# Two bias rows written into PSUM by ScalarE, and a reordered last stage, in a two-layer graph network kernel

## What is computed

```
xn = layernorm(x)
support = ((xn @ U) * s) @ Vt                                # rank 64
g  = relu(segment_sum(support[col] * val, row) + bias)       # L1_gnn_bias
q  = softmax over each head; k = softmax over the nodes
m  = (q @ (k^T v per head)) @ w_proj + b_proj                # L1_mix_b_proj
x  = x + g + m
ll, lh, hl, hh = haar(layernorm(x))
h  = gelu(interpolate(ll) @ fc1^T + fc1_b)
x  = x + inverse_haar(h @ fc2^T + fc2_b, lh, hl, hh)
```

## Time and profile before

| | |
|---|---|
| median of 3 runs | 594.62 us |
| the profiled execution | 594.25 us |
| its span, first to last instruction | 592.5 us |
| PE / DVE / ACT / POOL busy in it | 550.9 / 474.2 / 326.2 / 289.6 us |
| granted PE clock | full speed throughout (1.0) |

### The profile page before, as it was taken

The page is one execution under the profiler, slowest core; times in us unless marked ns, Lnnn a source line. Parts: engine busy times, 40 slices in busy tenths (PEclk is TensorE's granted clock), DMA queues, the critical chain, the costliest instruction groups (busy, mean ns, idle before and its releaser), DMA issues.

```text
span 592.5 us, 8690 instructions
## 1 busy us (share of the span) xinstructions
PE 550.9 (93%) x2921; PEld 443.8 (75%) x2921; DVE 474.2 (80%) x1037; ACT 326.2 (55%) x614; POOL 289.6 (49%) x321
## 2 busy tenths in 40 slices
PE   2988989998999999999999998999998999999997
PEld 1776877775877777888887665878876788778787
DVE  7689989888999778757898878768767786677996
ACT  7767868767764672122214765556436786423242
POOL 3747677676778705635661694000503565021553
PEclk9999999999999999999999999999999999999999
DMA  9400000000002020102204001000002000020004
GB/s 319 154 2 1 1 1 2 1 1 2 0 2 72 2 71 18 37 19 82 38 14 139 15 9 63 0 1 1 1 2 88 1 0 2 2 90 1 1 0 175
DMA packets 15046, 21.12 MB, mean 36 GB/s; under 512 B 3260, under 2 KB 6000, under 8 KB 15002
## 3 DMA queue, kind: packets, MB, share of 16 engines
q1 hardware_dynamic: 13674, 17.94, 9.6%
q10 hardware_dynamic: 1328, 2.62, 1.2%
HBM read 18.00 MB, written 2.56 MB: 35 GB/s over the span
## 4 chain that ended last, share of the span: by engine, by line
PE 58%; DVE 20%; issue 8%; POOL 6%; ACT 4%; DMA 3%; DVEq 1%; ACTq 0%; SPq 0%; POOLq 0%
PE p L2197 10%; PE pQ L2317 4%; PE p L2032 4%; PE p L2317 4%; DVE onehot L1374 3%; POOL qx L1183 2%; PE pH L2209 2%; PE pQ L2048 2%; DVE p L1472 2%; PE p L2282 2%; PE pQ L2515 2%; PE pH L2515 2%; PE pQ L2209 2%; PE pH L2048 2%; POOL xT L1171 2%
## 5 line engine op out<-in xcount | busy, mean ns | idle before, releaser
L999 POOL TENSOR_TENSOR Loh<-onehot,whl 128x512 fp32r<-128x512 f32 x85 | 89.4, 1052 | 47.6 <-DVE onehot L1374 47.6
L1374 DVE TENSOR_SCALAR onehot<-iota_src,srclo 128x128 fp32r<-128x128 f32 x170 | 74.7, 479 | 0.7 <-DVE flagint L1386 0.7
L2032 PEld LDWEIGHTS p<-Roh,Loh 128*128 128x128 f32 x340 | 47.6, 190 | 31.6 <-issue 27.7
L2197 PE MATMUL p<-G,ATs 128*128 128x512 f32 x300 | 70.5, 391 | 0.0
L2197 PEld LDWEIGHTS p<-G,ATs 128*128 128x128 f32 x300 | 55.9, 188 | 11.6 <-issue 0.2
L2032 PE MATMUL p<-Roh,Loh 128*128 128x200 f32 x340 | 53.2, 279 | 11.7 <-POOL Loh L999 4.9
L566 ACT ACTIVATE away<-iota_key,key 128x200 f32<-128x200 f32 x85 | 38.7, 456 | 24.2 <-PE p L2032 24.2
L2048 PE MATMUL pQ<-wsl,xT 128*128 128x512 f32 x168 | 47.5, 412 | 2.4 <-DVE xT L1288 2.4
L2048 PE MATMUL pH<-wsl,xT 128*128 128x512 f32 x168 | 45.4, 398 | 0.0
L568 ACT ACTIVATE Roh<-away,onesf 128x200 fp32r<-128x200 f32 x85 | 39.3, 463 | 2.8
L1405 DVE TENSOR_TENSOR AT<-AT,p 128x200 f32 x85 | 30.0, 353 | 13.2 <-PE p L2032 8.4
(11 more groups left out here) (650 smaller groups left out, 1440.7 us busy)
## 6 DMA issues: line engine op xcount, KB each, us to landing
xb<-in_x SPq DMA_DIRECT2D x9, 256.0 KB, 2.6
out<-nodes SPq DMA_DIRECT2D x9, 256.0 KB
wraw<-in_L_mix_w_qkv ACTq DMA_DIRECT2D x2, 1024.0 KB, 7.7
raw<-in_L_mix_w_qkv SPq DMA_DIRECT2D x2, 1024.0 KB, 5.2
nodes<-in_x SPq DMA_DIRECT2D x1, 1024.0 KB, 8.9
wraw<-in_L_mix_w_qkv SPq DMA_DIRECT2D x1, 1024.0 KB, 11.3
wraw<-in_L_gnn_W SPq DMA_DIRECT2D x1, 1024.0 KB, 13.5
raw<-in_L_mix_w_out SPq DMA_DIRECT2D x1, 1024.0 KB, 5.2
```

The costliest lines, as they stand in the source:

```text
L999: pool.tensor_tensor(Loh[:, g % SLOTS], o, w, ALU.mult).then_inc(S["oh_pool"], 1)
L1374: ins = v.tensor_scalar(onehot_[:, g % SLOTS, c, :], iota_src[:], srclo[:, 2 * g + c:2 * g + c + 1], None, ALU.is_equal)
L2032: ins = pe.matmul(pW[g % 2][:, 0:T * WIN], Loh[:, g % SLOTS, c, part, :], Roh[:, g % RSLOTS, c, :], start=(c + part == 0), stop=(c + part ...
L2197: ins = pe.matmul(pG[u][:, :], ATs[:, u, x, s_, :], G[:, y, s_, :], start=(s_ + n == 0), stop=(s_ == T - 1 and n == 2))
```

## The change

It does seven things, all in the second layer.

1. `b2` becomes a plain float32 tile with both bias rows on all 128 partitions, by two broadcast transfers of 256 KB in place of two of 4 KB. DVE's three preparing instructions and a POOL memset go.
2. The 4 bias matmuls behind `kT . Wp` and the 10 in `support` go. ACT copies a bias row into the PSUM bank (`support_bias`, `mix_bias`, 128x512, 10 of each), and the products accumulate on it (`start=False`). PE waits for these copies (`pg_ok`, `pm_ok`).
3. On ACT the copies of tile t+2 stand right behind `r2_hi(t + 2)`, and wait for `x3_ok` of tile t.
4. `gelu` of groups 1 and 2 writes back into its PSUM bank, and its doubling reads from there.
5. `doubled(0)` on ACT moves behind `sums_hi(1)`; `gelu_lo(0)` moves from DVE (before `sums_lo(1)`) to POOL, between pair_sums(8) and pair_sums(9), where `scaled_nodes(4)` stood; that one is now done with the later ones.
6. PE's order in the last stage becomes low(1), outer(0), inner(1), outer(1), outer(2), low(2), outer(3), inner(2), outer(4) to outer(9). DVE's order of the last stage stays.
7. The transposes of the key product (line 2469) clear a bank once instead of four times; as many instructions as before.

```diff
-                    [("vraw", [P, D]), ("b2", [P, 2, D], F32R)])
+                    [("vraw", [P, D]), ("b2", [P, 2, D])])
...
+        def grown(g, b):
+            n = min(4, T - 4 * g) * DH
+            return hf[:, b, 0:n] if g == 0 else hbank[g][:, b * HALF:b * HALF + n]
+
+        def doubled_lo(eng, g, b):
+            n = min(4, T - 4 * g) * DH
+            o = slice(8 * g * DH, 8 * g * DH + 2 * n)
+            return eng.tensor_tensor(hT[:, 1, b, o].rearrange("p (r v) -> p r v", v=2),
+                                     grown(g, b).rearrange("p (r v) -> p r v", v=1).broadcast_to([P, n, 2]),
+                                     hT[:, 0, b, o].rearrange("p (r v) -> p r v", v=2).bitcast(F32), ALU.subtract)
...
-                sp.dma_start(xn[0:2, k, :], a[name].partition_broadcast(2)).then_inc(S["ld_b2"], 16)
+                sp.dma_start(b2[:, k, :], a[name].partition_broadcast(P)).then_inc(S["ld_b2"], 16)
...
+            def support_bias(t):
+                if t < 2:
+                    act.wait_ge(S["ld_b2"], 32 + after["ld_b2"])
+                    act.wait_ge(S["zt_lo"], KC + after["zt_lo"])
+                else:
+                    act.wait_ge(S["x3_ok"], t - 1 + after["x3_ok"])
+                act.activation(pG[t % 2][:, :], b2[:, 0, :], ACT.Copy).then_inc(S["pg_ok"], 1)
+
+            def mix_bias(t):
+                if t < 2:
+                    act.wait_ge(S["mw_lo"], 2 + after["mw_lo"])
+                else:
+                    act.wait_ge(S["x3_ok"], t - 1 + after["x3_ok"])
+                act.activation(pM[t % 2][:, :], b2[:, 1, :], ACT.Copy).then_inc(S["pm_ok"], 1)
+
             r2_hi(0, 0, True)
+            support_bias(0)
+            support_bias(1)
             for p, bank in enumerate(wbank2):
...
+            mix_bias(0)
             r2_hi(1, 1, True)
+            mix_bias(1)
             for t in range(T):
                 if t + 2 < T:
                     r2_hi(t + 2, t % 2)
+                    support_bias(t + 2)
+                    mix_bias(t + 2)
...
                     gelu(0)
-                    doubled(0)
                 if t == 8:
                     sums_hi(1)
+                    doubled(0)
...
-            pool.memset(b2[:].bitcast(F32), 0.0).then_inc(S["c1"], 1)
...
             pair_sums(8)
-            scaled_nodes(4)
+            for b in range(2):
+                pool.wait_ge(S["hh_hi"], b + 1)
+                doubled_lo(pool, 0, b).then_inc(S["hh_lo0"], 1)
             pair_sums(9)
...
-            for t in range(5, T):
+            for t in range(4, T):
                 scaled_nodes(t)
...
-            v.wait_ge(S["ld_b2"], 32 + after["ld_b2"])
-            v.wait_ge(S["c1"], 7)
-            step(v.tensor_scalar(xn[0:2, 1, :], xn[0:2, 1, :], 1.0 / HEADS, None, ALU.mult))
-            step(v.tensor_copy(b2[0:2, :, :], xn[0:2, :, :]))
-            v.scalar_tensor_tensor(b2[0:2, :, :], b2[0:2, :, :].bitcast(F32), lomask[0:2, 0:1], xn[0:2, :, :], ALU.mult, ALU.add).then_inc(S["b2_ok"], 1)
...
-                if t == 8:
-                    gelu_lo(0)
...
-                    ins = pe.transpose(bank[:, b * P:(b + 1) * P], z[:, c * P:(c + 1) * P], ident[:])
+                    ins = pe.matmul(bank[:, b * P:(b + 1) * P], z[:, c * P:(c + 1) * P], ident[:], is_transpose=True,
+                                    start=(b == 0), stop=(b == 3), skip_group_check=True)
...
+                pe.wait_ge(S["pg_ok"], t + 1 + after["pg_ok"])
                 for n, (x, y) in enumerate(THREE):
-                    pe.matmul(pG[u][:, :], agT[:, x, t * P:(t + 1) * P], Vt[:, y, :], start=(n == 0), stop=False)
-                pe.matmul(pG[u][:, :], rows1[:, 0, :], b2[:, 0, :], start=False, stop=True).then_inc(S["s2_mm"], 1)
+                    ins = pe.matmul(pG[u][:, :], agT[:, x, t * P:(t + 1) * P], Vt[:, y, :], start=False, stop=(n == 2), skip_group_check=True)
+                ins.then_inc(S["s2_mm"], 1)
...
                 pe.wait_ge(S["r2_lo"], t + 1 + after["r2_lo"])
+                pe.wait_ge(S["pm_ok"], t + 1 + after["pm_ok"])
...
-                pe.matmul(bank[:, :], kT[:, p, :], Wp[:, p, :], start=True, stop=False)
-                if p == 0:
-                    pe.wait_ge(S["b2_ok"], 1)
-                pe.matmul(bank[:, :], rows1[:, 0, :], b2[:, 1, :], start=False, stop=True).then_inc(S["mw_mm"], 1)
+                pe.matmul(bank[:, :], kT[:, p, :], Wp[:, p, :], start=True, stop=True).then_inc(S["mw_mm"], 1)
...
             outer(0)
+            inner(1)
             outer(1)
-            inner(1)
             pe.wait_ge(S["x3_ok"], T + after["x3_ok"])
             outer(2)
+            low(2)
             outer(3)
-            low(2)
-            outer(4)
-            outer(5)
             inner(2)
-            for t in range(6, T):
+            for t in range(4, T):
                 outer(t)
```

More of the change, by code:

```diff
@@ L157, in build @@
                     [("N0", [P, 2, 2, 20]), ("hin", [P, FFL, REM + 1], F32R), ("st3", [P, T, 3, 6]),
-                     ("pairs", [P, P]), ("rows1", [P, 2, P], F32R),
+                     ("pairs", [P, P]), ("rows1", [P, 1, P], F32R),
                      ("wt16", [P, 4, 16]), ("iota16", [P, 16]), ("pairm", [P, P], F32R),
@@ L908, in gelu @@
                 n = min(4, T - 4 * g) * DH
-                r = slice(4 * g * DH, 4 * g * DH + n)
                 act.wait_ge(S["hh_mm"], g + 1)
                 for b in range(2):
-                    act.activation(hf[:, b, r], hbank[g][:, b * HALF:b * HALF + n], ACT.Gelu, bias=fb1[:, b:b + 1]).then_inc(S["hh_g"], 1)
+                    act.activation(grown(g, b), hbank[g][:, b * HALF:b * HALF + n], ACT.Gelu, bias=fb1[:, b:b + 1]).then_inc(S["hh_g"], 1)
             def doubled(g):
                 n = min(4, T - 4 * g) * DH
-                r = slice(4 * g * DH, 4 * g * DH + n)
                 act.wait_ge(S["hh_g"], 2 * g + 2)
@@ L2506, in support @@
                     pe.wait_ge(S["x3_ok"], t - 1 + after["x3_ok"])
+                pe.wait_ge(S["pg_ok"], t + 1 + after["pg_ok"])
                 for n, (x, y) in enumerate(THREE):
-                    pe.matmul(pG[u][:, :], agT[:, x, t * P:(t + 1) * P], Vt[:, y, :], start=(n == 0), stop=False)
-                pe.matmul(pG[u][:, :], rows1[:, 0, :], b2[:, 0, :], start=False, stop=True).then_inc(S["s2_mm"], 1)
+                    ins = pe.matmul(pG[u][:, :], agT[:, x, t * P:(t + 1) * P], Vt[:, y, :], start=False, stop=(n == 2), skip_group_check=True)
+                ins.then_inc(S["s2_mm"], 1)
             def mix2(t, u):
                 pe.wait_ge(S["r2_lo"], t + 1 + after["r2_lo"])
+                pe.wait_ge(S["pm_ok"], t + 1 + after["pm_ok"])
                 for c in range(KC):
                     for n, (x, y) in enumerate(THREE):
-                        ins = pe.matmul(pM[u][:, :], xT[:, u, x, c, :], MW[:, y, c, :], start=(c + n == 0), stop=(c == KC - 1 and n == 2))
+                        ins = pe.matmul(pM[u][:, :], xT[:, u, x, c, :], MW[:, y, c, :], start=False, stop=(c == KC - 1 and n == 2), skip_group_check=True)
                 ins.then_inc(S["m2_mm"], 1)
@@ L2583, in outer @@
                     pe.wait_ge(S["o_ok"], t - 3)
-                pe.matmul(o, rows1[:, 1, :], b3[:, :], start=True, stop=False)
+                pe.matmul(o, rows1[:, 0, :], b3[:, :], start=True, stop=False)
                 for x in range(2):
                     pe.matmul(o, pairm[:], shl[:, x, t, :], start=False, stop=False)
-                pe.wait_ge(S["hh_lo"], 2 * (t // 4) + 2)
+                if t < 4:
+                    pe.wait_ge(S["hh_lo0"], 2 + after["hh_lo0"])
+                else:
+                    pe.wait_ge(S["hh_lo"], 2 * (t // 4))
                 for hb in range(2):
```

19 lines of the change are left out of this document (7 added, 12 removed).

## The result

After the change the median is 598.64 us (596.58 to 600.19, 13 runs), beside 595.83 (594.19 to 597.19, 13 runs) for the kernel before on the same chip. The ratio is 1.005 [1.0038, 1.0062], so the change costs 3.0 us (2.3 to 3.7). The forecast was +1.4 us and 596.0 us, with 598.2 as the upper end of the range. The sign was right, the size was not, and the median lies above the range. The profiled execution took 598.78 us with a span of 597.0.

What follows compares the result with a forecast made beforehand. It took PE, busy 93%, to bound the kernel except where ACT or DVE ends a wait. 0 until 571.25, then -0.2 + 0.1 + 1.55 = +1.4 us on 594.25 gave 595.65, plus 0.37 made 596.0 us; range 594.0 to 598.2.

Steps and rivals of the forecast that it cites:

- The lead lost at the W1 split: ACT's W1 split: bias copies ahead of it leave 0.1 of PE's 2.3 us of lead.
- the lower bound: Price of an ACT bias copy: about 0.45 us at least, 0.62 at most; 0.60 taken, nearer the lower end expected.
- The wait at tile 7: PE ahead of support(7): waits for ACT's bias copy, 0.7 us late.
- the repayment: Tiles 7 to 9: three more removed bias matmuls bring the 0.7 us back to 0 by the last mix product.
- The handover to low(1): Start of the last stage: sums_lo(1) no longer waits for gelu_lo(0), so low(1) starts 0.2 us earlier.
- POOL's two subtractions: Doubled halves for outer(0): twice 1.29 us, 1.69 at worst, done at 574.2 to 575.0; PE wants them at 574.5.
- The slower rival: Copies at upper bound, slow POOL subtractions, DVE and POOL interfering: +2.0 to +3.2 us, decided by outer(0)'s wait over 0.4; chance 0.32.
- The waits of the last stage: PE after low(1): waits 0.35 before inner(1), 0.6 before low(2), 0.6 before inner(2), together 1.55 us.
- 0.1 for POOL: Early last stage: 0.1 us allowed for PE waiting on POOL's doubled halves.
- the median of before 0.37 above the profiled execution: Base of the forecast: the median of the runs stands 0.37 us above the profiled execution, turning 595.65 into 596.0 us.

Runs made afterwards that it cites:

- late_copies: The changed kernel with only ACT's bias copies moved to later places in its order, at most tiles behind the splits and sums_hi; 596.08 us, ratio 0.9984 to before.
- after_filler: The changed kernel plus four unread 512-column matmuls between the last mix product and low(1); 596.87 us, ratio 1.0015 to before.
- bias_only: The kernel before plus parts 1 to 3 and the transposes (part 7); gelu, doubling and PE's order as before; 599.89 us, ratio 1.0069.
- dve_order: The changed kernel with DVE's sums_lo(2) ahead of result(1), and gelu_lo(1) and low_lo(2) ahead of result(2); 597.34 us, ratio 1.0020 to before.
- order_only: The kernel before with part 6 alone, PE's new order of the last stage; 597.44 us, ratio 1.0024.
- before_filler: The kernel before plus five unread 512-column matmuls between the last mix product and low(1); 594.88 us, ratio 0.9983.
- late_old_filler: late_old_order plus four unread 512-column matmuls between the last mix product and low(1); 593.63 us, ratio 0.9964 to before.
- doubling_only: The kernel before with parts 4 and 5 alone, the gelu and doubling parts; 594.96 us, ratio 0.9975.
- late_old_order: late_copies with PE's last stage in the order of the kernel before; 594.98 us, ratio 0.9987 to before.
- late_bias_only: late_old_order without parts 4 and 5, so the bias copies alone in their late places; 596.79 us, ratio 1.0024 to before.
- the five filled kernels: Before, after, bias_only, order_only and late_old_order, each plus four to nine unread matmuls ahead of low(1); ratios to before 0.9983, 1.0015, 1.0027, 1.0019, 0.9964.
- bias_filler: bias_only plus nine unread 512-column matmuls in its hole ahead of low(1); 597.65 us, ratio 1.0027 to before.

## Why the prediction was wrong

**The lead lost at the W1 split: right.** Forecast 0.1 of 2.3 us left, the split 0.1 earlier; it was 0.13 later. Most of that difference is ahead of the copies: r2_hi(5) starts 25.98 from the first turn, 0.19 later than forecast. A copy takes 0.60 and costs 0.52 of ACT's queue, where I had 0.50. The Trainium skill says that ScalarE reaches PSUM faster than SBUF ("ScalarE: Activation LUTs", "Step-by-step: what each stage is for"). In the rows this is about 0.02 us of 0.62, and the copies did not come near the lower bound. The forms of ACT, beside the earlier trace rows (count, busy us, mean ns, idle before):

```profile
L909 ACT ACTIVATE p<-b 128x512 f32<-128x512 f32 x10 | 5.9, 598 | 3.6 <-DVE nodes L1937 3.6
```

That it was the place on ACT is shown by late_copies, 2.05 us earlier at this point.

**The wait at tile 7: the right place and releaser, mis-sized.** Forecast 0.7 late, measured 1.19. sums_hi(0) started 2.49 later instead of 2.2, sums_lo(0) took 1.30 instead of 1.21 and began 0.1 behind ACT's end. I had let this wait be repaid by three more bias matmuls that are gone, "the last mix product ends when it did". It ended 0.54 later: of 1.19, 0.65 was repaid, which is about those three matmuls (0.69). So the repayment was as forecast and the debt was not.

**The handover to low(1): the right releaser, the wrong sign, off by 0.6.** Forecast -0.2, measured +0.44, from the same debt; sums_lo(1) took 1.33 instead of 1.21 and began at 54.25 from the first turn, where it stood at 53.92. POOL's two subtractions did not hold up outer(0), which runs on behind low(1) without a wait. The timeline of POOL after:

```profile
573.70 2.99 POOL L284 TENSOR_TENSOR hT<-hf,hT 128x512 fp32r<-128x512 f32 x2 [0.24 <-ACT hT L949]
```

That is 2.99 for two, where I had counted twice 1.29. The view of this line on POOL (count, then min/median/max in ns) shows that the two are unlike:

```profile
L284 POOL TENSOR_TENSOR hT<-hf,hT x2: 1159/1514/1868, 573.7 to 575.5; 128x512 fp32r<-128x512 f32 x2
```

The first, which began while DVE was at sums_lo(1), took 1.87; the second, with no such neighbour, 1.16. So the meeting cost POOL 0.71 us. The Trainium skill has a rule that the two engines hold one port in turn, each for its whole length ("SBUF — State Buffer", "Who interferes with whom"). By it POOL stands until DVE is through at 574.54, for 0.84 us; the trace agrees but for 0.13. The price stayed hidden: POOL was through at 576.69, and PE came for the halves at 576.84. The slower rival has +2.0 to +3.2, which holds the measured +3.0, but it was to decide by a wait of outer(0) over 0.4, and there was no such wait. Its time was near by luck.

**The waits of the last stage: the sum right at full clock, one of the three waits not there.** Forecast 0.35, 0.6 and 0.6 by which the stage becomes 1.55 longer, and 0.1 for POOL. At full clock (after_filler) inner(1) waits 0.36 and low(2) 0.74, but no wait is shown ahead of inner(2), nor in the kernel after. Counted from the start of the six matmuls ahead, which without a wait are followed by the next start 0.72 later, PE loses 0.52, 0.91 and 0.15 us at the three places. The stage is 1.74 longer than before, so the sum came out near because the first two losses were larger and made up for the third.

**Against equal clocks** the sum was thus 0.6 short: after_filler's 596.67 (7 executions at a mean clock of 1.0) against 594.67 (9) of before is +2.0, forecast +1.4. Most of this is the debt of tile 7, mis-sized by 0.5 and carried to the end. Taken apart at full clock, the copies cost 1.6 up to low(1) and 0.2 behind it, the order 1.5, and the gelu part gives back 0.95 (593.75 against 594.70). That is +2.4 beside +2.0 for all together; I did not trace the 0.4 between them.

**The term that was missing: PE's granted clock.** I read "full speed throughout" in the profile before and took PE's matmuls as constants. That is the step that failed worst, and it failed twice. Of the 3.0 us that the change costs, 0.8 to 1 goes with it. And I put the median of before 0.37 above the profiled execution, going by three runs; that execution had full clock, which only 9 of 35 have, and the median of 13 runs is 595.83, 1.6 above it. The forecast of 596.0 us was thus 2.6 us low: 1.2 by the base, 0.6 by the queues and 0.8 by the falls that the change adds. The clock is also why bias_only is slower than the whole change: its hole is 2.29 us and its low stretch twice as long, and filled it comes down to 1.0027. Open is what decides in a given execution. The kernel before has a hole of 1.31 and dve_order one of 1.25, and their profiles show no fall in the last stage, while order_only with 1.32 shows one. The early hole of 1.73, the same in all 14 profiles, is followed by a fall in four. So the length of the hole alone does not decide. before_filler gains 0.17% on before, at the edge of its interval, and its mean clock is higher (0.9986 against 0.9970), so some of the executions of before probably fell as well.

**A version that beats both.** late_old_filler keeps the copies (moved behind what DVE waits for) and the gelu parts, takes the old PE order and fills the hole: 593.63 us (592.21 to 594.41, 12 runs), 0.9964 [0.9947, 0.9981] of the kernel before. How much of this the bias copies bring is less sure: doubling_only, which has none of them and no filler, is at 0.9975 [0.9961, 0.9990], and the intervals overlap. In executions at a mean clock of 0.999 or more late_old_filler takes 592.2 (3), 2.1 less than before in its session, where doubling_only gains 0.95 in its own.

## What to carry to other kernels

Work taken from the busiest engine is worth its time only if the engine that takes it over does it behind the instructions that the chain waits for; here the same ten pairs of copies were worth 2.5 us more a few places further down ACT's list. A reorder on one engine has to be matched on the others: PE's new order met DVE's old one, and 0.8 us of its 1.7 was that mismatch. And a PE hole can cost more than its length, so judge variants at equal granted clock, and consider matmuls that nobody reads where the hole can't be closed.

## What the runs showed of the hardware

The granted clock fell to half, 1.2 GHz, for 3.4 or 6.8 us in kernels whose PE is busy 93% of the span, 0.6 to 2.9 us after the end of a hole of 1.22 us (after), 1.08 (late_copies), 1.07 (late_old_order), 1.32 (order_only), 2.29 (bias_only) or 2.25 (late_bias_only). It did not fall behind a hole of 1.31 (before) or 1.25 (dve_order), nor in any profile whose wait there was 0.16 to 0.29 us (the five filled kernels and doubling_only). Behind the hole of 1.73 us at 78 us it fell in 4 of 14 profiles. In the last stage a fall of 3.4 us cost 0.75 to 1.5 us, one of 6.8 us 3.05 (bias_only against bias_filler).

ScalarE's copy of 128x512 float32 from SBUF into PSUM takes 0.60 us, the next instruction starting 0.52 behind it. In after, a load of ACT's function tables took 1.28 us (from 547.09), the activation ahead of it ended at 547.07, and the next one started at 548.38.

A GpSimd subtraction of 128x512 with its operands in SBUF took 1.16 us alone and 1.75 to 2.15 us where a VectorE subtraction of two SBUF operands was under way when it started. In six profiles (after, after_filler, dve_order, doubling_only, late_copies, late_old_filler) the added time, 0.59 to 0.99 us, follows the time left to the end of VectorE's instruction, 0.73 to 1.13 us, at 0.13 to 0.15 less.
